# One layer-norm step per tile on VectorE instead of two, x2f one iteration earlier, and weight casts spread over 28 tiles instead of 32

## The reference

```python
# attention part, per group of 256 tokens
normed = (x - mu) * rsqrt(var + 1e-5) * norm_g + norm_b
hv     = silu(normed @ W_h + b_h);  v, gate = hv[:, :2048], hv[:, 2048:]
qk     = silu(normed @ W_qk + b_qk)            # 128 wide
quad_q, lin_q, quad_k, lin_k = qk * gamma[h] + beta[h]
attn   = relu(quad_q @ quad_k.T / 256 + rel_pos_bias) ** 2
lin_kv = lin_k.T @ v / n                        # over all 4096 tokens
out    = gate * (attn @ v + lin_q @ lin_kv)
x2     = layernorm(x + (out @ W_o + b_o + x))
# feed-forward part
y      = relu(x2 @ W1 + b1) @ W2 + b2
result = layernorm(x2 + y)
```

## Time and profile before

| | |
|---|---|
| runs (us) | 2865.63, 2594.97, 2597.55; median 2597.55 |
| profiled execution: time | 2597.5 us |
| profiled execution: span, slowest core (core 5) | 2595.9 us |
| spans of the eight cores | 2579.4 to 2595.9 us |
| mean granted TensorE clock of the cores | 0.930 to 0.934 of 2.4 GHz |
| TensorE matmul busy | 2058.7 us (79%) |
| ScalarE busy | 773.5 us (30%) |
| VectorE busy | 535.3 us (21%) |
| DMA traffic | 256.27 MB, mean 99 GB/s |

### The profile page before, as it was taken

One profiled execution on the slowest core, in us unless ns is written; L12 is line 12 of the kernel. 1 busy time (PEld: TensorE's weight loads), 2 busy tenths in 40 slices (PEclk: granted clock), 3 DMA queues, 4 the chain that ended last, 5 costly groups with the idle time before them and its releaser, 6 DMA issues.

```text
span 2595.9 us, 28168 instructions; the slowest of 8 cores (2579.4 to 2595.9 us)
## 1 busy us (share of the span) xinstructions
PE 2058.7 (79%) x9498; PEld 880.6 (34%) x9498; DVE 535.3 (21%) x1118; ACT 773.5 (30%) x1256; POOL 96.8 (4%) x178
## 2 busy tenths in 40 slices
PE   0258999999999366767666666999999989898988
PEld 0113333333333132333333332434343434343433
DVE  0211222222211224333333330011111101010202
ACT  0344344444433122222222232222223131313131
POOL 1000111111111000000000000000000000000000
PEclk9879999999999688888888888999999999999999
DMA  9713655555454845454545424312020202020101
GB/s 157 130 34 96 148 127 127 120 141 127 111 110 111 248 131 155 132 147 130 147 138 150 124 90 144 94 38 60 22 65 17 65 17 69 13 73 25 41 25 49
DMA packets 125203, 256.27 MB, mean 99 GB/s; under 512 B 57629, under 2 KB 66150, under 8 KB 123016
## 3 DMA queue, kind: packets, MB, share of 16 engines
q1 hardware_dynamic: 80792, 129.40, 16.5%
q10 hardware_dynamic: 27648, 92.29, 12.0%
q0 software_dynamic: 16624, 32.79, 9.5%
HBM read 188.64 MB, written 112.20 MB: 116 GB/s over the span
## 4 chain that ended last, share of the span: by engine, by line
PE 76%; DVE 6%; ACT 6%; DMA 5%; issue 5%; SPq 1%; DVEq 0%; ACTq 0%
PE E L639 19%; PE E L811 17%; PE E L794 16%; PE E L762 9%; PE E L723 3%; PE E L636 3%; ACT h L1052 2%; PE E L727 2%; ACT wh L906 2%; DVE sums L1277 1%; PE E L828 1%; PE E L658 1%; PE E L741 1%; DVE x2bf L1288 1%; DMA w<-w1bf_sp 1%
## 5 line engine op out<-in xcount | busy, mean ns | idle before, releaser
L794 PE MATMUL E<-xfm,w 128*128 128x512 bf16 x2048 | 461.2, 384 | 75.8 <-ACT h L1052 60.3
L639 PE MATMUL E<-wh,nfm 128*128 128x512 bf16 x2048 | 506.0, 392 | 0.0
L811 PE MATMUL E<-w,h 128*128 128x512 bf16 x2048 | 453.2, 379 | 0.0
L794 PEld LDWEIGHTS E<-xfm,w 128*128 128x128 bf16 x2048 | 198.3, 99 | 337.2 <-issue 113.6
L811 PEld LDWEIGHTS E<-w,h 128*128 128x128 bf16 x2048 | 195.1, 98 | 241.2 <-issue 14.6
L639 PEld LDWEIGHTS E<-wh,nfm 128*128 128x128 bf16 x2048 | 183.1, 100 | 253.5 <-issue 80.6
L1052 ACT ACTIVATE h<-E,b_fm 128x512 bf16<-128x512 f32 x256 | 173.5, 686 | 320.7 <-PE E L794 320.7
L762 PE MATMUL E<-wo,gfm 128*128 128x512 bf16 x1024 | 238.6, 387 | 0.0
L1317 DVE TENSOR_TENSOR pre<-E,x2r 128x1024 f32<-128x1024 f32 x32 | 39.2, 1224 | 866.6 <-PE E L811 866.6
L636 PE MATMUL E<-bh_eff_bf,ones 1*128 1x512 bf16 x256 | 100.3, 392 | 89.1 <-ACT vt L888 45.2
L828 PE MATMUL E<-ident,x2bf 128*128 128x128 bf16 x256 | 32.4, 306 | 167.8 <-DVE x2bf L1288 166.9
(11 more groups left out here) (110 smaller groups left out, 1237.9 us busy)
## 6 DMA issues: line engine op xcount, KB each, us to landing
g_sp<-gt ACTq DMA_DIRECT2D x64, 512.0 KB, 3.9
g<-g_sp ACTq DMA_DIRECT2D x64, 512.0 KB, 7.1
xt<-x SPq DMA_DIRECT2D x32, 512.0 KB, 6.1
v_sp<-vt SPq DMA_DIRECT2D x32, 512.0 KB, 3.7
v<-v_sp SPq DMA_DIRECT2D x32, 512.0 KB, 5.0
x2t<-x SPq DMA_DIRECT2D x32, 512.0 KB, 4.3
x_sp<-x2f ACTq DMA_DIRECT2D x32, 512.0 KB, 6.8
x2r<-x_sp SPq DMA_DIRECT2D x32, 512.0 KB, 5.4
```

The lines of the kernel that those rows point to most:

```text
L639: mm = tn.matmul(pslc, T["nfm"][:, sl2 + c * 128:sl2 + (c + 1) * 128], T["wh"][:, c * 2 * HID + s * 512:c * 2 * HID + (s + 1) * 512], star ...
L794: mm = tn.matmul(ps, T["w1"][:, dc * 4096 + ci * 128:dc * 4096 + (ci + 1) * 128], T["xfm3"][:, (Ti % 2) * 4 * DM + dc * 512:(Ti % 2) * 4 * ...
L811: mm = tn.matmul(ps, T["h1"][:, ci * 512 + tt * 128:ci * 512 + (tt + 1) * 128], T["w2"][:, ci * DM + h * 512:ci * DM + (h + 1) * 512], sta ...
```

## The change

Three things are changed. (1) The precasts are dealt out over tiles 0 to 27: NPT is 28, so 64 precasts give two or three per tile, and the last four tiles have none. (2) On ACT, `p2_x2f` is called for tile tau-2 instead of tau-3, and the extra call for tile NT-3 behind the loop goes. (3) On DVE, `p2_pre2ln_a` and `p2_pre2ln_b` become one function, called for tile tau-1: behind the reciprocal of tile u, DVE waits for the square root of the same tile u and then makes nms and x2bf of u, where it made those of u-1 before. PE's and SP's lists are unchanged, as is ACT's place for the square root.

```diff
-            for k in range(t * 64 // NT, (t + 1) * 64 // NT):
+            NPT = max(NT - 4, 1)
+            for k in range(min(t, NPT) * 64 // NPT, min(t + 1, NPT) * 64 // NPT):
                 precast(k)
@@ ScalarE, stage 2
-            p2_x2f(tau - 3)
+            p2_x2f(tau - 2)
             p2_ln2sq(tau - 1)
         _emit_xfmev(sc, NT - 3)
         p2_sqrt(NT - 2)
         p2_gfmev(NT - 1)
-        p2_x2f(NT - 3)
         p2_ln2sq(NT - 1)
@@ VectorE, stage 2
-        def p2_pre2ln_a(u):
+        def p2_pre2ln(u):
...
             wge(ve, "c_sqst", NT + u + 1)
             smalls_a(u, 1).then_inc(S["c_v2a"], 1)
-
-        def p2_pre2ln_b(u):
-            if not (0 <= u < NT):
-                return
             wge(ve, "c_s2a", u + 1)
             smalls_b(u, 1).then_inc(S["c_v2b"], 1)
             vsync()
...
             p2_gated(tau)
-            p2_pre2ln_a(tau - 1)
-            p2_pre2ln_b(tau - 2)
-        p2_pre2ln_a(NT - 1)
-        p2_pre2ln_b(NT - 2)
-        p2_pre2ln_b(NT - 1)
+            p2_pre2ln(tau - 1)
+        p2_pre2ln(NT - 1)
```

## The result

The changed kernel takes 2426.7 us (median of 8 runs, 2425.85 to 2430.01) where the kernel before took 2594.47 in the runs beside it. The ratio is 0.9356 with a 95% interval of 0.9345 to 0.9366: 168 us or 6.4% less. Forecast were 2438 us, with a range of 2409 to 2490. The profiled execution took 2421.94 us with a span of 2420.4, against 2597.5 and 2595.9: these two spans lie 175.5 us apart, more than the 168 of the medians, since the profiled execution after was shorter than all eight runs and the one before longer than most of its own. Each kernel also has some executions that take up to 14% longer at a lower granted clock on one die or both (2716.82 us for one of the changed kernel); times are medians of all executions, the ratios leave these out.

A forecast was written before the change was run, and what follows sets the result against it. TensorE, the busiest engine, was held by 5.34 us stalls for x2bf, queued late on DVE, and the slow clock behind them. Gain 155.0 + 4 = 159 us from 2597.5 gives 2438 us, range 2409 to 2490.

The forecast's parts named there:

- The walk from E: Stage 2, one iteration from the end of Wo's matmuls (E) to the next: 13.62 us odd, 16.01 even, before clock price.
- The clock: TensorE in stage 2: slow matmuls behind stalls cost 1.9 us per even iteration, 0.2 us per odd one.
- the 3.5 us stall: Even iterations: TensorE waits about 3.5 us for gfm copies, as relu ahead of them waits for simb behind x2bf.
- The lower bound, 1.36 us: Even iterations' clock price from below: Wo took 9.18 us instead of 7.82 after a 1.76 us stall.
- the 2.6 us: Even iterations' clock price from above: the slow clock's cost after the 5.34 us stall for x2bf.
- The strict reading of the Trainium skill: TensorE's clock: a gap shorter than the 5.34 us ones might cost nothing, giving 2409 us.
- The sum: Stage 2: 29 iterations fall from 613.0 to 458.0 us; with 4 us from the last Wo, gain 159, giving 2438 us.
- Edits taken at nothing: Precasts in 28 tiles and ScalarE's x2f one iteration earlier: each taken as 0 gain and 0 cost.
- That odd iterations stall like even ones: Rival in stage 2: all 29 iterations take 17.91 us, gain 98, 2500 us; chance 0.12.
- That transfers are the bound: Rival in stage 2: a 150 GB/s ceiling makes iterations 19.3 us, gain 56, 2541 us; chance 0.08.
- v late: Rival: TensorE waits for v at the start of each even iteration; 2659 us if v lands in 26 us; chance 0.04.
- The signs named beforehand: Stage 2: x2bf wait nearly gone, gfm wait about 66 us, nms waits every iteration, iterations alternate about 13.8 and 17.9 us.

The follow-up runs named there:

- the filler run: Changed kernel with 14 useless 128x512 matmuls per even iteration 2 to 28, between the second and third group of transposes; 2409.88 us, ratio 0.9279.
- the run with relu late: Changed kernel with ScalarE's relu of even iterations moved behind the four gfm copies; 2372.99 us, ratio 0.9148.
- the run with more bytes: Changed kernel with one more 512 KB DRAM to DRAM transfer per iteration of stage 2, issued by SP; 2430.08 us, ratio 0.9361.
- the run with four more operations: Changed kernel with mu computed four more times in VectorE's statistics of stage 2, ahead of the others; 2470.45 us, ratio 0.9520.
- the second part first: Kernel before with VectorE doing the layer norm's second part (tile tau-2) ahead of its first part (tile tau-1); 2391.88 us, ratio 0.9220.

## Why the prediction was right

*The walk from E.* It was made with durations of the trace of before and gave the places of all that follows. Measured against it: reciprocal to square root 0.25, to nms 0.63, to x2bf 0.81 us, as reckoned. Stall of even iterations 3.33 us (forecast 3.5), of odd ones 0.89 and 0.30 (forecast 1.1). Odd iteration 13.46 us (13.82 with its clock), even one without a fall of the clock 15.90 (16.01). The walk had the reciprocal, the square root and x2bf at the very places where they came. It was too long by 0.16 us in odd iterations, where the copies follow the square root's start by 0.13 us and 0.30 was taken, and by 0.11 in even ones, most of it because simb starts 0.72 us after x2bf's start and 0.81 was taken.

*The clock.* 1.9 us per even iteration was taken between two bounds; the filler run shows 1.8. For odd iterations 0.2 us was taken and 0 measured. That the clock would fall behind the 3.5 us stall was argued from rows and came true in 13 of 13 cases; that the size came out so close is in part luck. The lower bound, 1.36 us, was read from an iteration in which the clock had fallen behind a stall of 1.76 us. It did so in three of the 13 even iterations from 4 to 28 of the trace before (10, 16 and 26). Iteration 24 is one of the ten others, in which the first matmul of Wo kept its 0.39 us:

```profile
1388.13 0.87 PE L741 MATMUL E<-ident,gtm 128*128 128x128 bf16 x8 [1.76 <-ACT gfm L991]
1388.93 0.39 PE L757 MATMUL E<-bo_bf,ones 1*128 1x512 bf16 x1
```

So the bound from below was 0, and halfway from there to the 2.6 us would have been 1.3. Single even iterations of the changed kernel paid from 1.3 to 3.2 us.

The strict reading of the Trainium skill (TensorE: Matmul & The Clock Gate, "HAM oscillation — how this bites in real kernels"), by which these gaps might have been free, was rightly set aside: without the clock's price the sum would have been 2409 us, and the filler run shows that the price is there.

*The sum.* The forecast of 2438 us started from the 2597.5 of the profiled execution, 3 us above the median before; a gain of 159 us was forecast and 168 measured. 29 iterations took 447.0 us, forecast 458.0. The 11 us split into 15 odd iterations (202.6 instead of 207.3, 4.7 us), 13 even ones at 17.75 instead of 17.91 (2.1 us), and iteration 30, which was counted as even at 17.9 us and took 13.66 (4.3 us). The last is an oversight: there is no seventeenth group, so in iteration 30 no relu stands ahead of the gfm copies, and in the trace before its stall was 0.65 us already. The iteration of the last Wo gained 3.0 us, not 4 (16.1 instead of 19.1), since its transposes wait for the xfmt copies and Wo follows at half clock:

```profile
1379.59 0.61 PE L742 MATMUL E<-ident,gtm 128*128 128x128 bf16 x8 [2.89 <-ACT xfmt L1077]
...
1382.09 0.60 PE L758 MATMUL E<-bo_bf,ones 1*128 1x512 bf16 x1
```

The remaining 3.4 us behind that Wo and the 3.1 us before iteration 2 are within the scatter of single executions. From the end of the last Wo to the end of the span the kernel before took 1031.4 us and the changed kernel 1028.0, but the run with relu late, whose lists are the same there, took 1031.8. Iteration 2 ended between 924.9 and 932.4 us in the traces of this study.

*Edits taken at nothing.* The precasts are shown to be nothing within about 3 us. x2f's place is within the uncertainty of some 6 us; ScalarE ended x2f 10.6 us behind E in an even and 10.2 in an odd iteration (12 and 9 reckoned), ahead of its next duty in both.

*The rivals.* That odd iterations stall like even ones: no, because only relu, an even affair, stood behind the longer DVE queue. That transfers are the bound: out by 221 GB/s with relu late and by the run with more bytes. v late: the one long wait for v or lq is still that of 28.3 us at the start of the stage. The signs named beforehand came as said: x2bf is waited for nowhere, nms waits in every iteration, the wait of line 741 (now 742) comes to 61.9 us (66 forecast), and iterations of 13.5 us alternate with ones of 17.2 to 19.1. The rate over the 29 iterations was 188 GB/s (some 180 forecast), since they were shorter.

## What to carry to other kernels

When a stall is due to a result that was ready to be made earlier, ask on which engine it queued, and move it ahead of the work that it doesn't depend on; joining it to its own tile's chain works too, but puts a round trip to another engine, and the operation itself, ahead of the engine's next work (here that choice cost 35 of the 203 us that the mere change of order gives). When a stall is to be removed, walk one iteration with the measured durations to find what is late next: here it was the relu of even iterations, put ahead of the copies for which TensorE waits, and moving it was worth 54 us. Price a stall of TensorE twice, once for its length and once for the slow matmuls behind it, and count in how many iterations of the trace the slow matmuls really follow.

## What the hardware showed that was not expected

Matmuls whose result is thrown away made the kernel 17 to 20 us faster, by holding the granted clock at 0.97 instead of 0.93 in the same stretch of the slowest core (0.96 to 0.99 on the eight cores, instead of 0.91 to 0.93).

And the same stall does not always cost the same. Two stalls of 0.30 and 0.89 us with short transposes between them left the clock up in all such odd iterations of the changed kernel. With the filler it fell in five odd iterations, in three of them behind just these two stalls and in the two others behind slightly longer ones; with relu late it fell in two of 29, behind 0.65 and 0.89 us and behind 0.30 and 1.09. Nor does the longer stall always cost more: 1.93 us or more left the clock up in all fifteen odd iterations of the run with four more operations, where 1.97 us lowered it in six of 13 even ones with the second part first, and 1.76 us in three of 13 before the change. A fall behind a stall of up to 2 us cost 1.6 to 1.7 us in the runs with the filler, with relu late and with the second part first. So the length of a stall alone does not decide it. What does isn't settled by these runs, and a stall of 1 to 2 us can be priced only with a range, here 0 to 1.7 us on top of its length.
